# TensorE's order in a graph kernel: the fourth group's sum placed inside the linear layer, and the picked rows ahead of the self rows' transposes

## The chip, the cores and the metric

The kernel runs on one core of a Trainium2 chip. The metric is the device time of one execution in microseconds, the median of several runs. Five engines work side by side from their own instruction streams and meet at semaphores: TensorE (PE), VectorE (DVE), ScalarE (ACT), GpSimd (POOL) and SyncE (SP, which here issues DMAs). Matmuls write PSUM, which DVE and ACT read.

## The reference

One layer of a graph network over 6,250 nodes with 128 features, 106,250 edges, three edge types and three node types.

```python
parts = [relu(x)]
for t in range(3):                                  # edge types
    msg = relu(x[src] @ W_e[t].T + b_e[t])
    msg = where(edge_type == t, msg, 0)
    parts.append(segment_sum(msg, dst, 6250))
agg = concatenate(parts, axis=1)                    # 6250 x 512
for t in range(3):                                  # node types
    updated = where(node_type == t, agg @ W_n[t].T + b_n[t], updated)
out = layernorm(x + updated + x)
```

The edges come sorted by `dst`; among them is one edge from each node to itself (a "self" edge).

## The kernel before, in words

A first stage (until some 110 us) computes the message of every node under every edge type, `relu(x @ W_e[t].T + b_e[t])`, and stores the 18,750 rows in DRAM as `message_table`. After it the edges are worked off in 45 iterations `j`. An iteration holds two rows of 1,080 sorted edges; most of their messages are fetched from the table by indirect DMA, 128 rows at a time, in 14 columns that form four groups of 3, 4, 3 and 4 columns.

For a group `g` of iteration `j` the engines do this:

- POOL issues the group's gathers (line 619), one per column, into `msg` (which the trace calls `tab`). The buffer is single: the gathers of group `g` for iteration `j + 1` wait until TensorE has summed group `g` of iteration `j` (`group_summed`). POOL issues them in the order of the groups.
- DVE makes the one-hot matrices of the group for the next iteration (`one_hot`, line 1116, output `work`), also after `group_summed`, and then adds the group's sum from PSUM to the accumulator (`add_sums`, line 1125, output `acc`).
- TensorE multiplies messages by one-hot (`sum_group`, line 1516), one matmul per column, into one of two PSUM banks (`AGG`), so a sum waits until the last but one was added.

Other work is laid between these sums on TensorE. The "picked rows" are edges whose source lies in a narrow range of nodes; instead of a gather they are picked from resident rows by a one-hot matmul. `dense_turn` (line 1533, ten matmuls in two sets of five) picks them, DVE multiplies by type masks (`dense_mask`, line 1204, output `order_f`), `dense_make` (lines 1546 and 1548) makes their messages, ACT applies relu (line 747), `dense_sum` (line 1555) sums them. The "early" edges (iterations up to 35) are turned (`early_turn`, 1486), made (1496) and summed (1506).

The tile of nodes that is complete is finished one or two iterations later. `finish_turn` (1577) transposes its 128 rows of `x` into a PSUM bank; ACT writes their relu to `stage` (761); `place_selfs` (1570) transposes the three types of self rows into the same bank once ACT has read it (`stage_xt`); DVE adds them to the accumulator's sums in `stage` (1269). The linear layer is `linear_open` (a bias matmul, 1586, and the part of relu(x), 1587) and `linear_types` (1595, one matmul of 384 columns for each edge type). DVE then selects by node type, adds and normalizes (`finish_h`, 1238 to 1246, and `finish_y`, 1252 and 1254).

The order on each engine is the order in which the code is written; nothing is scheduled at run time. On TensorE it is `iteration(j)` in the tensor block (lines 1604 to 1683), with `FIN = 2` and `NG = 4`, so `g == FIN + 1` is the fourth group. SP's stream (loads for the next tiles, stores) and POOL's, DVE's and ACT's are not touched by the change.

Of the kernel before, what the change touches and what calls it, by code (L numbers as in the profile page):

```python
# [35 lines left out]
N, D, T, E = 6250, 128, 3, 106250  # L36
# [29 lines left out]
FIN = 2  # L66
# [74 lines left out]
def build(nc, x, src, dst, etype, ntype, w_e, b_e, w_n, b_n, out):  # L141
# [5 lines left out]
    with ExitStack() as ctx:  # L147
# [1266 lines left out]
        def _(pe):  # L1414
# [158 lines left out]
            def finish_turn(tile, nth, loads, z=0, first=False):  # L1573
                pe.wait_ge(fin_x[z], 16 * loads)
                if not first:
                    pe.wait_ge(stage_xt[z], nth)
                pe.transpose(ps[:, FIN_XT_PS[z], 0:P], xg[:, at(tile), :].rearrange("p a d -> p (a d)"), ident[:, :]
                             ).then_inc(fin_xt[z], 1)
# [10 lines left out]
            def linear_types(nth, z, first=1, last=T):  # L1589

                lin = ps[:, LIN_PS[z], 0:T * D]
                if first == 1:
                    pe.wait_ge(stage_acc[z], nth + 1)
                for i in range(first, last + 1):
                    ins = pe.matmul(lin, stage[z][:, i, :], wn_t[:, i, :], start=False, stop=(i == T))  # L1595
                if last == T:
                    ins.then_inc(fin_lin[z], 1)
# [5 lines left out]
            def iteration(j, early=False, fin=True, extra=None, last=False, loads=None):  # L1603
                start = j == 1
                for g in range(NG):
# [57 lines left out]
                    if g == FIN:  # L1663
                        if j == 2:
                            dense_sum(2)
                        if j > 1:
                            linear_open(j - 2, first=j == 2)
                            linear_types(j - 2, 0, 1, T)
                        if fin:
                            finish_turn(j - 1, j - 1, loads, first=start)  # L1670
                        if extra is not None:
                            linear_types(extra, 1)
                    if g == FIN + 1 and fin and j > 1:
                        place_selfs(j - 1, j - 1)
                    if g == FIN and j == 1:
                        dense_turn(1)
                    if g == FIN + 1:
                        if j == 1:
                            spread_types()
                            dense_make(1)  # L1680
                            dense_sum(1)
                        if j > 1:
                            dense_turn(j + 1)

            pe.wait_ge(consts_set, 1)
# [13 lines left out]
            for j in range(1, NI - 1):  # L1699
                iteration(j, j < NE, extra=j - EXTRA_AT if EXTRA_AT <= j < EXTRA_AT + KE else None,  # L1700
                          loads=batches_up_to(j - 1))
# [38 lines left out]
```

## Time and profile before

| | |
|---|---|
| three runs | 1091.16 us median, 1078.62 to 1099.07 |
| span of the profiled execution | 1076.0 us (from its first to its last instruction; no other time is given for it) |
| busy: PE, DVE, POOL, ACT | 72%, 64%, 62%, 14% |
| gathers by POOL in the 45 iterations | 630, 943 ns each |
| mean granted clock of TensorE | 0.872 |

In the timeline rows the columns are start in us, duration in us, engine and line, operation, output and inputs, count, and in square brackets the idle time of the engine before the row with what ended it. "issue" is time without a wait that the profile shows, "remote" a releaser that it could not name. An fp32 matmul stands there as two records, so x8 are the four matmuls of a group of four columns. A matmul's end is modelled.

### The profile page before, as it was taken

The numbers are of one execution on the slowest core, as the hardware profiler recorded it, in microseconds if no ns is written. First come the engines' busy times: TensorE is split into PE (matmuls) and PEld (weight loads), VectorE is DVE, ScalarE is ACT, GpSimd is POOL, SyncE is SP. The second block draws the span as 40 slices with busy tenths as digits, with TensorE's granted clock in tenths as the row PEclk, the third lists the DMA queues.
The fourth block names the chain that finished last, engine by engine and source line by source line (L and its number), as shares of the span: only waits on it lengthen the run. The fifth ranks groups of instructions, "written<-read, shape, count | busy, mean of one in ns | idle before, by whom it ended". The sixth has DMA issues, their size and how long they took to land. (4 is left out here: it accounts for less than half of the span.)

```text
span 1076.0 us, 13097 instructions
## 1 busy us (share of the span) xinstructions
PE 771.1 (72%) x4200; PEld 611.8 (57%) x4200; DVE 683.5 (64%) x1539; ACT 149.6 (14%) x397; POOL 671.4 (62%) x718
## 2 busy tenths in 40 slices
PE   5574267777778778777676686888787786778866
PEld 3242156666666566566555565666566565566654
DVE  7997866666555656656566565656656654465645
ACT  2264101101101101100110110011011001111101
POOL 7776655666566666665666665666666666665660
PEclk9697578978898998998999988989888978898898
DMA  7476312422222223223223223223223233132320
GB/s 219 135 256 190 81 50 60 86 72 67 78 80 75 71 77 85 72 70 89 71 70 93 74 67 91 71 67 96 72 67 108 71 105 90 45 93 70 87 57 16
DMA packets 65777, 94.03 MB, mean 87 GB/s; under 512 B 16497, under 2 KB 49233, under 8 KB 65711
## 3 DMA queue, kind: packets, MB, share of 16 engines
q0 software_dynamic: 22432, 45.99, 17.2%
q1 hardware_dynamic: 40577, 43.14, 13.0%
q10 hardware_dynamic: 2702, 4.08, 1.3%
q8 instruction: 34, 0.56, 0.2%
q14 instruction: 32, 0.26, 0.1%
HBM read 80.23 MB, written 12.92 MB: 87 GB/s over the span
## 5 line engine op out<-in xcount | busy, mean ns | idle before, releaser
L619 POOL DMA_INDIRECT tab<-message_table,idx_t x630 | 594.3, 943 | 353.0 <-issue 170.4
L1116 DVE TENSOR_TENSOR work<-key_t,ps 128x378 f32<-128x378 f32 (+1 forms) x180 | 109.5, 610 | 253.1 <-remote 133.0
L1516 PE MATMUL ps<-work,tab 128*128 128x126 f32 x1260 | 197.4, 304 | 35.4 <-DVE acc L1125 20.6
L1516 PEld LDWEIGHTS ps<-work,tab 128*128 128x128 f32 x1260 | 183.3, 219 | 50.3 <-DVE acc L1125 25.5
L1546 PE MATMUL ps<-we_t,order_f 128*128 128x128 f32 x540 | 115.4, 368 | 123.2 <-DVE order_f L1204 84.1
L1546 PEld LDWEIGHTS ps<-we_t,order_f 128*128 128x128 f32 x540 | 93.3, 255 | 135.6 <-DVE order_f L1204 88.8
L1595 PE MATMUL ps<-wn_t,stage 128*128 128x384 f32 x294 | 104.6, 493 | 0.0
L1204 DVE TENSOR_TENSOR order_f<-ps,dst_raw 128x768 f32<-128x768 f32 x45 | 43.1, 957 | 71.7 <-remote 56.7
L615 POOL DMA_INDIRECT xg<-in_x,esrc_t x67 | 71.0, 1060 | 23.9 <-issue 17.7
L1595 PEld LDWEIGHTS ps<-wn_t,stage 128*128 128x128 f32 x294 | 56.3, 193 | 39.7 <-issue 3.1
L747 ACT ACTIVATE dense_f<-ps 128x256 f32<-128x256 f32 x45 | 17.2, 383 | 432.7 <-PE ps L1548 228.8
L1496 PE MATMUL ps<-we_t,xst 128*128 128x384 f32 x142 | 60.7, 554 | 20.0 <-issue 19.6
L1125 DVE TENSOR_TENSOR acc<-ps,acc 128x126 f32 x216 | 61.1, 283 | 9.3 <-PE ps L1516 8.1
L1533 PE MATMUL ps<-first_wide,tab 128*128 128x128 f32 x450 | 59.1, 279 | 4.6 <-issue 2.9
L1448 PE MATMUL ps<-we_t,work 128*128 128x384 f32 x98 | 44.7, 541 | 19.0 <-issue 10.4
L1533 PE MATMUL ps<-dense_f,tab 128*128 128x128 f32 x450 | 58.1, 277 | 0.0
L1533 PEld LDWEIGHTS ps<-first_wide,tab 128*128 128x128 f32 x450 | 54.8, 195 | 5.5 <-issue 5.5
L1241 DVE SCALAR_TENSOR_TENSOR h<-ps,mask,h 128x128 f32<-128x128 f32 x147 | 51.6, 351 | 6.2 <-PE ps L1595 0.9
L1533 PEld LDWEIGHTS ps<-dense_f,tab 128*128 128x128 f32 x450 | 54.5, 194 | 0.0
L1555 PE MATMUL ps<-first_wide,dense_f 128*128 128x216 f32 x180 | 45.9, 382 | 5.2 <-ACT dense_f L747 5.2
L1496 PEld LDWEIGHTS ps<-we_t,xst 128*128 128x128 f32 x142 | 26.7, 209 | 35.5 <-issue 26.6
L1555 PEld LDWEIGHTS ps<-first_wide,dense_f 128*128 128x128 f32 x180 | 36.8, 214 | 16.8 <-ACT dense_f L747 6.3
(231 smaller groups left out, 952.2 us busy)
## 6 DMA issues: line engine op xcount, KB each, us to landing
tab<-message_table,idx_t POOLq DMA_INDIRECT x630
message_table<-tab SPq DMA_DIRECT2D x24, 384.0 KB
dst_raw<-dense_types SPq DMA_DIRECT2D x45, 192.0 KB
wn_raw<-message_table SPq DMA_DIRECT2D x22, 384.0 KB
src_wide<-dense_lists SPq DMA_DIRECT2D x45, 128.0 KB
xg<-in_x SPq DMA_DIRECT2D x11, 256.0 KB
work<-in_x ACTq DMA_DIRECT2D x10, 256.0 KB
out<-xg SPq DMA_DIRECT2D x10, 256.0 KB
```

What stands on the lines that cost most here:

```text
L615: pool.indirect_dma_start(xg[:, q, :], None, x, bass.IndirectOffsetOnAxis(ap=rows, axis=0)).then_inc(x_gathered, 16)
L619: pool.indirect_dma_start(msg[:, slot, :], None, table, bass.IndirectOffsetOnAxis(ap=rows, axis=0)).then_inc(signal, 16)
L1116: dve.tensor_tensor(hot[:, first:first + n, :].rearrange("p c (t w) -> p c t w", w=WIN), keys.broadcast_to((P, n, T, WIN)), iota_win.rearr ...
L1125: dve.tensor_tensor(cols, sums_bank(nth).rearrange("p (t c) -> p t c", t=T), cols, ALU.add).then_inc(added, 1)
L1241: fin_link(dve.scalar_tensor_tensor(h[z][:, :], ps[:, LIN_PS[z], t * D:(t + 1) * D], mask[:, t, at(tile)], h[z][:, :], ALU.mult, ALU.add), ...
L1448: pe.matmul(ps[:, MSG_PS + i, 0:T * D], xt[:, par, i, :], we_t[:, :], start=True, stop=False)
L1496: ins = pe.matmul(ps[:, E_MSG_PS[c], 0:T * D], xst[:, c, :], we_t[:, :], start=True, stop=True)
L1516: ins = pe.matmul(sums_bank(nth), msg[:, column, :], hot[:, column, :], start=(c == 0), stop=(c == n - 1))
L1533: ins = pe.matmul(dxt_ps[:, :, s * DENSE:(s + 1) * DENSE], dx[:, (SETS - 1 - s) * DT + k, :], donehot[s][:, k, :, :], start=(k == 0), stop ...
L1546: pe.matmul(dmsg_ps[:, side, :], dxm[:, side, t, :], we_t[:, t * D:(t + 1) * D], start=(t == 0), stop=False)
L1555: ins = pe.matmul(dense_sums(side), dsel[:, side, :], dhot[:, side, :], start=True, stop=True)
L1595: ins = pe.matmul(lin, stage[z][:, i, :], wn_t[:, i, :], start=False, stop=(i == T))
```

## The change

For `j > 2` and all but the last iteration it moves instructions on TensorE and does nothing else. The number of instructions stays the same.

```diff
                         if j > 1:
                             linear_open(j - 2, first=j == 2)
-                            linear_types(j - 2, 0, 1, T)
-                        if fin:
+                            linear_types(j - 2, 0, 1, T if j == 2 else 1)
+                        if fin and j < 3:
                             finish_turn(j - 1, j - 1, loads, first=start)
                         if extra is not None:
                             linear_types(extra, 1)
+                    if g == FIN + 1 and j > 2:
+                        linear_types(j - 2, 0, 2, T)
+                        finish_turn(j - 1, j - 1, loads)
+                        dense_turn(j + 1)
                     if g == FIN + 1 and fin and j > 1:
                         place_selfs(j - 1, j - 1)
...
-                        if j > 1:
+                        if j == 2:
                             dense_turn(j + 1)
```

TensorE's stream from the linear layer's first type to the next iteration's first sum (the wait on `gathered3` opens the fourth group's sum, the one on `gathered0` the next first group's; the words in brackets are semaphores), before:

```order
L1595 MATMUL ps<-wn_t,stage 128x384 [waits stage_acc0]
L1595 MATMUL ps<-wn_t,stage 128x384 x2
L1577 MATMUL ps<-ident,xg 128x128 [waits stage_xt0,fin_x0]
L1516 MATMUL ps<-work,tab 128x126 [waits gathered3,added]
L1516 MATMUL ps<-work,tab 128x126 x3
L1570 MATMUL ps<-ident,wn_raw 128x128 [waits stage_xt0,self_masked0]
L1570 MATMUL ps<-ident,wn_raw 128x128 x2
L1533 MATMUL ps<-first_wide,tab 128x2x64 [waits d_onehot,d_added]
L1533 MATMUL ps<-first_wide,tab 128x2x64 x4
L1533 MATMUL ps<-dense_f,tab 128x2x64 [waits d_onehot]
L1533 MATMUL ps<-dense_f,tab 128x2x64 x4
L1516 MATMUL ps<-work,tab 128x126 [waits gathered0,added]
```

The same place of the changed kernel:

```order
L1595 MATMUL ps<-wn_t,stage 128x384 [waits stage_acc0]
L1516 MATMUL ps<-work,tab 128x126 [waits gathered3,added]
L1516 MATMUL ps<-work,tab 128x126 x3
L1595 MATMUL ps<-wn_t,stage 128x384 x2
L1577 MATMUL ps<-ident,xg 128x128 [waits stage_xt0,fin_x0]
L1533 MATMUL ps<-first_wide,tab 128x2x64 [waits d_onehot,d_added]
L1533 MATMUL ps<-first_wide,tab 128x2x64 x4
L1533 MATMUL ps<-dense_f,tab 128x2x64 [waits d_onehot]
L1533 MATMUL ps<-dense_f,tab 128x2x64 x4
L1570 MATMUL ps<-ident,wn_raw 128x128 [waits stage_xt0,self_masked0]
L1570 MATMUL ps<-ident,wn_raw 128x128 x2
L1516 MATMUL ps<-work,tab 128x126 [waits gathered0,added]
```

The fourth sum moved ahead of two matmuls of the linear layer and one transpose; the picked rows' ten matmuls moved ahead of the three transposes of the self rows. In all 41 changed iterations the piece reads like this. The streams of DVE, ACT, POOL and SP are the same.

## Rows read from the trace of the kernel before

**Rows 1.** The page, head and part 1: busy time (share) xinstructions of each engine.

```profile
span 1076.0 us, 13097 instructions
...
PE 771.1 (72%) x4200; PEld 611.8 (57%) x4200; DVE 683.5 (64%) x1539; ACT 149.6 (14%) x397; POOL 671.4 (62%) x718
```

**Rows 2.** Waits: engine line, waited for: us in total, times, longest.

```profile
DVE work L1116 <- remote: 133.0, 48, 4.4
DVE work L1116 <- PE ps L1516: 117.3, 42, 4.6
POOL tab L619 <- remote: 98.5, 55, 3.3
```

**Rows 3.** Timeline of POOL around two stops, 720 to 737 us.

```profile
723.63 0.94 POOL L619 DMA_INDIRECT tab<-message_table,idx_t  x1 [1.80 <-remote]
...
731.12 0.94 POOL L619 DMA_INDIRECT tab<-message_table,idx_t  x1 [0.30 <-issue]
733.81 0.94 POOL L619 DMA_INDIRECT tab<-message_table,idx_t  x1 [1.75 <-PE ps L1516]
```

**Rows 4.** Timeline of PE, 720 to 738 us.

```profile
727.20 2.10 PE L1595 MATMUL ps<-wn_t,stage 128*128 128x384 f32 x6
729.13 0.27 PE L1577 MATMUL ps<-ident,xg 128*128 128x128 f32 x1
729.24 1.05 PE L1516 MATMUL ps<-work,tab 128*128 128x126 f32 x8
730.13 0.49 PE L1570 MATMUL ps<-ident,wn_raw 128*128 128x128 f32 x3
730.46 1.28 PE L1533 MATMUL ps<-first_wide,tab 128*128 128x128 f32 x10
...
732.69 0.83 PE L1516 MATMUL ps<-work,tab 128*128 128x126 f32 x6
```

**Rows 5.** Timeline of DVE, 722 to 738 us.

```profile
726.26 0.29 DVE L1125 TENSOR_TENSOR acc<-ps,acc 128x126 f32 x1
...
729.53 0.81 DVE L1195 TENSOR_TENSOR dense_f<-src_wide,ps 128x640 f32<-128x640 f32 x1
733.57 0.68 DVE L1116 TENSOR_TENSOR work<-key_t,ps 128x504 f32<-128x504 f32 x1 [3.23 <-PE ps L1516]
...
735.07 0.96 DVE L1204 TENSOR_TENSOR order_f<-ps,dst_raw 128x768 f32<-128x768 f32 x1 [0.62 <-remote]
...
736.60 0.54 DVE L1269 TENSOR_TENSOR stage<-acc,ps 128x384 f32<-128x384 f32 x1
```

**Rows 6.** Timeline of ACT, 722 to 738 us.

```profile
729.44 0.28 ACT L761 ACTIVATE stage<-ps 128x128 f32<-128x128 f32 x1 [1.99 <-PE ps L1577]
```

**Rows 7.** Timeline of PE, 505 to 518 us: a second sum.

```profile
510.73 1.05 PE L1516 MATMUL ps<-work,tab 128*128 128x126 f32 x8
```

**Rows 8.** Timeline of POOL, 508 to 517 us.

```profile
516.32 0.94 POOL L619 DMA_INDIRECT tab<-message_table,idx_t  x1 [1.76 <-remote]
```

**Rows 9.** Timeline of POOL, 319 to 320 and 460 to 464 us.

```profile
319.26 0.94 POOL L619 DMA_INDIRECT tab<-message_table,idx_t  x1 [1.76 <-remote]
...
462.63 0.94 POOL L619 DMA_INDIRECT tab<-message_table,idx_t  x1 [1.82 <-PE ps L1516]
```

**Rows 10.** Timeline of POOL, 476 to 507 us: a short stop and three long ones.

```profile
481.68 0.94 POOL L619 DMA_INDIRECT tab<-message_table,idx_t  x1 [0.33 <-remote]
...
488.99 0.94 POOL L619 DMA_INDIRECT tab<-message_table,idx_t  x1 [2.61 <-remote]
...
495.94 0.94 POOL L619 DMA_INDIRECT tab<-message_table,idx_t  x1 [3.51 <-PE ps L1516]
...
506.13 0.94 POOL L619 DMA_INDIRECT tab<-message_table,idx_t  x1 [1.76 <-remote]
```

**Rows 11.** Timeline of DVE, 478 to 491 us.

```profile
481.44 0.68 DVE L1116 TENSOR_TENSOR work<-key_t,ps 128x504 f32<-128x504 f32 x1 [1.82 <-remote]
...
488.68 0.96 DVE L1204 TENSOR_TENSOR order_f<-ps,dst_raw 128x768 f32<-128x768 f32 x1 [6.36 <-remote]
```

## The prediction, made before the changed kernel ran

> **What bounds the kernel now.** I read the page first: no engine is full, PE is busy 72% of the 1076.0 us and POOL 62% [rows 1]. Next the waits: DVE's one-hots of line 1116 wait 133.0 us for a releaser without a name and 117.3 us for TensorE's sums, and POOL's gathers wait another 98.5 us in 55 stops [rows 2]. So the kernel is bound by a ring of signals between POOL, PE and DVE. What the ring costs is read from the timelines of one ordinary iteration.
>
> The iteration takes 20.48 us: POOL's gathers behind the fourth sum start at 319.26 and, seven iterations later, at 462.63 [rows 9]. POOL issues seven gathers at a pitch of 1.25 us ((731.12 - 723.63) / 6), ends them at 732.06, stands still for 1.75 us and starts again at 733.81; the stop before was 1.80 us [rows 3]. Two series and two stops make an iteration. The first stop ends with the second group's sum, the other with the fourth group's.
>
> The fourth sum is the point of the change. TensorE shows it at 729.24 for 1.05 us, so ended at 730.29 [rows 4]. DVE, free since 730.34, takes up the one-hot that waits for it only at 733.57 [rows 5], and POOL goes on at 733.81 [rows 3]. Between the shown end of the sum and its effect lie 3.28 us. For the transpose just ahead of it there is no such gap: it ends at 729.40 and ACT starts on its result at 729.44 [rows 4, 6]. So what is late is the signal (or the real end) of the sum, and the question is what holds it.
>
> **What the change does, part by part.** All in one iteration, 41 times, on the rows of TensorE [rows 4].
>
> The sum moves ahead of two of three types and one transpose. The three types take 729.13 - 727.20 = 1.93 us, two of them 1.29, the transpose 0.11 (729.24 - 729.13): the sum starts at 727.84 and is shown ended at 728.89, 1.40 us earlier. Nothing holds its start: the addition that frees its bank ends at 726.55 [rows 5], 1.29 us before.
>
> The other types and `finish_turn` come later by the sum's 0.89 us (730.13 - 729.24). DVE reads the linear layer only after the next iteration's second sum, some ten us later: no cost. The transpose is shown at 730.02 and ACT's copy takes 0.28 us [rows 6], so `stage` would be there at about 730.6.
>
> The picked rows end earlier by the 0.33 us of `place_selfs` (730.46 - 730.13), and `place_selfs` follows at 732.36; DVE reads it at 736.60 [rows 5]. Ahead of it now stands a wait on ACT's copy with 1.7 us in hand. Behind that wait is queued the next first sum, shown at 732.69 as before. If the transpose's signal were held as the fourth sum's is, until about 733.57, `place_selfs` would wait to 733.9 and the first sum would end near 734.9; its reader on DVE stands behind the mask that ends at 736.03 [rows 5], so I take 0. That mask is the cover. If it were gone, the wait would cost up to 1.2 us (733.9 - 732.69), 49 us in 41 iterations; nothing here gains.
>
> The picked rows' mask starts at 735.07, 0.62 us after DVE is free [rows 5]; 0.33 us of it may go. It feeds the second sum, whose stop is the other one.
>
> What then is 1.40 us on the fourth sum worth? The bound on one side: POOL's stop goes from 1.75 to the usual 0.30 between gathers, 1.45 us, times 41 is 59 us. On the other side nothing, if the signal doesn't follow the sum. The nearest row decides for nothing. At 510.73 TensorE ran a second group's sum unusually early, shown ended at 511.78 [rows 7], and POOL started only at 516.32, after a stop of 1.76 us [rows 8]. There 4.54 us lie between the end of the sum and POOL's start, at 730.29 and 733.81 it was 3.52 us, yet the stops are 1.76 and 1.75 us [rows 3, 8]. A sum that was done a microsecond earlier shortened nothing: the signal seems to come at a fixed time after POOL's own series of seven gathers has ended. I take 0 for the sum's move.
>
> The Trainium skill ("Perfetto Trace Analysis", Per-instruction lifecycle, Tensor Engine Instruction) says that the shown end of a matmul is an estimate and that its semaphore update follows the write's acknowledgement, outside of the shown window. The transpose's 0.04 us agrees, the fourth sum's 3.28 us shows how far outside it may be. By that rule alone the signal belongs to the matmul and moves with it, which is the first rival below.
>
> The sum: 0 for the fourth sum, 0 for the moved transposes, at most a few tenths in single iterations at the end, where TensorE itself is late: about -1 us. Against the profiled execution: 1076.0 - 1 = 1075. The median of the runs is 15.2 us above that span (the fastest run 2.6 us), so 1090 us in the runs' measure.
>
> **The rivals.**
>
> *The signal follows the sum* (faster). Then DVE makes the fourth one-hot right at 730.34, POOL loses its stop, and the picked rows' mask can start when `dense_turn` is done instead of at 735.07, so that the second sum keeps up. Full price 59 us: 1032. The second stop would grow by part of it where DVE and TensorE can't follow, since TensorE's sequence up to the first sum is as long as before; with half to all of the 1.45 us I take 45 us: 1046. For it: the names in the waits, TensorE's sum as POOL's releaser; and that the sum would now stand earlier in the series of gathers (5.3 us after its start at 723.63) than any held one I looked at, while the transpose at 5.8 us passed at once [rows 3, 4, 6]. Against it: rows 7 and 8. Chance 0.30.
>
> *The signal gets through too early, and later ones are held longer* (slower). In one place the trace shows what happens when POOL does not stop after seven: at 481.68 it went on after 0.33 us and issued four more gathers, then stood 2.61 and 3.51 us [rows 10]; the picked rows' mask came 7.24 us after the fourth one-hot (488.68 - 481.44) [rows 11] instead of 1.50 (735.07 - 733.57) [rows 5]. From 462.63 to 506.13 two iterations took 43.50 us [rows 9, 10] against 40.96 for two ordinary ones: 2.54 us lost. The price is that, and it decides as soon as the fourth sum's signal comes within the 8.4 us of the series. In every second changed iteration it is 20 x 2.54 = 51 us: 1142; in one of four 25 us: 1116. For it: an earlier sum makes just this likelier. Against: it has to be frequent to count. With the 1.2 us of a wait in front of `place_selfs` in some iterations it is about the same size. Chance 0.24.
>
> *The forecast*: the stops stay, within 2%. Chance 0.46.
>
> **How the numbers follow.** About 2%, 22 us, is what a measurement of this kernel can tell from no change (its three runs span 20 us). Faster by over 2% (under 1069) takes the first rival, 0.30; slower (over 1113) the second, 0.24; between them 0.46. The range for 8 in 10 runs from 1042, which leaves out the first rival's last part down to 1032, to 1130, which takes in the second with an occurrence in one of three iterations. The forecast's own range is 1075 to 1105, that of the runs before.
>
> **What would show it.** In the profile after: POOL's stops behind the fourth sum still 1.7 to 1.9 us and the fourth one-hot still waiting, now some 4.7 us after the shown end of its sum: right. Those stops down to 0.3 us, with iterations of 19 us: the first rival. Series of eleven gathers without a stop, followed by stops over 2.5 us and a mask 5 us or more behind the fourth one-hot: the second. An idle TensorE ahead of line 1570 would show that ACT's copy is late and the cover thin. Most of all the prediction would be wrong if what I read as held by POOL's series were only TensorE's own lateness.

## The result: 4.4% slower, and the profile after

Median after 1142.72 us (1130.19 to 1152.82, 4 runs), before 1093.63 us (1078.62 to 1099.07, 4 runs), ratio 1.0439, 95% interval 1.0379 to 1.0499. Two of after's four runs (1148.03 and 1152.82 us) belong to a slower state of the chip with a lower granted clock, and the ratio leaves them out; the other two took 1130.19 and 1137.42 us. The forecast was 1090 us and its range ended at 1130; the slower rival gave 1142. The profiled execution grew from 1076.0 to 1128.4 us. First the page of after, its head and its line of busy times [rows 1]:

```profile
span 1128.4 us, 13097 instructions
...
PE 799.5 (71%) x4200; PEld 641.1 (57%) x4200; DVE 684.2 (61%) x1539; ACT 150.3 (13%) x397; POOL 671.8 (60%) x718
```

DVE and POOL did the same work to a microsecond. PE ran the same 4200 instructions in 28 us more, at a mean granted clock of 0.819 against 0.872. So for POOL and DVE the 52.4 us are waiting. First one wait of before, then the waits of after (us in total, times, longest), and the page's group of POOL's gathers, of before and then of after:

```profile
DVE order_f L1204 <- remote: 56.7, 32, 6.4
```

```profile
DVE order_f L1204 <- remote: 218.0, 38, 8.8
ACT stage L761 <- remote: 213.1, 30, 10.4
POOL tab L619 <- PE ps L1516: 136.0, 48, 10.6
PE ps L1546 <- DVE order_f L1204: 123.4, 37, 6.6
```

```profile
L619 POOL DMA_INDIRECT tab<-message_table,idx_t x630 | 594.3, 943 | 353.0 <-issue 170.4 <-remote 98.5 <-PE ps L1516 80.1
```

```profile
L619 POOL DMA_INDIRECT tab<-message_table,idx_t x630 | 594.4, 943 | 400.8 <-issue 173.7 <-PE ps L1516 136.0 <-remote 91.1
```

POOL idles 47.8 us more: that is nearly all of the 52.4. Where, its timeline shows. In one iteration of after, number 33, the gathers run from 867.06 to 880.47 without a stop:

```profile
867.06 0.94 POOL L619 DMA_INDIRECT tab<-message_table,idx_t  x1 [3.36 <-PE ps L1516]
...
879.53 0.94 POOL L619 DMA_INDIRECT tab<-message_table,idx_t  x1 [0.30 <-issue]
883.13 0.94 POOL L619 DMA_INDIRECT tab<-message_table,idx_t  x1 [2.66 <-remote]
...
890.04 0.94 POOL L619 DMA_INDIRECT tab<-message_table,idx_t  x1 [3.47 <-PE ps L1516]
```

That is a series of eleven gathers (a "series" is a row of gathers 0.30 us apart, a "stop" the longer gap behind it), a stop of 2.66 us, three gathers, a stop of 3.47 us, where before had seven, 1.80, seven, 1.75 [rows 3]; 22.98 us against 20.48. It is the pattern of rows 10. I counted the series in POOL's timelines (a gap over 0.56 us ends one): before has 5 of eleven and 74 of seven, after 21 of eleven and 35 of seven.

The loss is not spread over the 41 changed iterations. I counted POOL's gathers off against the iterations: POOL reaches the second group of iteration 16 at 456.17 us, 3.8 us later than in before (452.38), that of iteration 35 at 890.04, 43.5 us later (846.58), and the last one's 51.5 us later. From iteration 10 to 16 after keeps before's time, but not its pattern: the stops of its two series of seven stand behind the first and the third group's sums, no longer behind the second and the fourth. Iteration 10 begins at 329.57, and these are its third group's first gather and the next iteration's first:

```profile
339.86 0.94 POOL L619 DMA_INDIRECT tab<-message_table,idx_t  x1 [1.86 <-PE ps L1516]
...
350.04 0.94 POOL L619 DMA_INDIRECT tab<-message_table,idx_t  x1 [1.75 <-remote]
```

From iteration 17 to 37 nearly every one is long, some 23 us. The first of this row begins with three gathers and a stop of 3.17 us behind a second sum that took 1.91 us (477.44 to 479.35), and only then comes a series of eleven (479.62). So a series of eleven and a late second sum seem to bring each other about; which comes first is not the same everywhere (in before, at 472.92, it was the eleven).

TensorE in iteration 33 [rows 4]:

```profile
871.27 1.05 PE L1516 MATMUL ps<-work,tab 128*128 128x126 f32 x8
872.16 1.46 PE L1595 MATMUL ps<-wn_t,stage 128*128 128x384 f32 x4
873.45 0.27 PE L1577 MATMUL ps<-ident,xg 128*128 128x128 f32 x1
...
874.68 1.28 PE L1533 MATMUL ps<-dense_f,tab 128*128 128x128 f32 x10
878.83 0.52 PE L1570 MATMUL ps<-ident,wn_raw 128*128 128x128 f32 x3 [2.87 <-ACT stage L761]
...
883.78 1.65 PE L1546 MATMUL ps<-we_t,order_f 128*128 128x128 f32 x6 [3.77 <-DVE order_f L1204]
...
887.85 1.91 PE L1516 MATMUL ps<-work,tab 128*128 128x126 f32 x8
```

And its readers on DVE and ACT [rows 5, 6]:

```profile
874.85 0.68 DVE L1116 TENSOR_TENSOR work<-key_t,ps 128x504 f32<-128x504 f32 x1 [1.08 <-remote]
878.40 0.28 ACT L761 ACTIVATE stage<-ps 128x128 f32<-128x128 f32 x1 [7.53 <-remote]
882.77 0.96 DVE L1204 TENSOR_TENSOR order_f<-ps,dst_raw 128x768 f32<-128x768 f32 x1 [7.04 <-remote]
```

Three results of TensorE reach their readers late. The fourth sum, shown ended at 872.32, is taken up at 874.85 (2.53 us, of which DVE was busy for all but the last 1.08), in the middle of POOL's series, so POOL is free to issue on. The transpose of `finish_turn` is shown ended at 873.72, ACT starts at 878.40 (4.68 us). The picked rows are done at 875.96, and the mask starts at 882.77, 6.81 us later and 2.30 us behind the end of the eleven. The iteration is that chain: 13.41 us of series (867.06 to 880.47), 2.30 to the mask, 7.27 from the mask to POOL's start at 890.04 behind the second sum; together 22.98. In before the same chain, from the mask at 735.07 to the end of the second sum at 740.94, lies under seven gathers (733.81 to 742.24); here only three are left to cover it. Its second sum in before:

```profile
739.89 1.05 PE L1516 MATMUL ps<-work,tab 128*128 128x126 f32 x8
```

One row more, of the stretch behind the mask in after (columns: us, busy us and instructions of PE, PEld, DVE, ACT, POOL, then the granted clock, DMA share, GB/s):

```profile
883.00:890.00 7.00, 6.22 (x27) 5.54 (x28) 5.43 (x9) 0.77 (x2) 2.83 (x3) 0.50 0.10 28
```

Granted clock 0.50, the 1.2 GHz level, after TensorE stood idle for 3.77 us: the second sum takes 1.91 us instead of 1.05 in before. From the mask's start to the second sum's end it is 6.99 us here (882.77 to 889.76) and 5.87 in before, for the same instructions. An estimate from these rows: 1.12 of the 2.50 us that an iteration loses are the clock's, since here that chain lies open, and the rest is waiting for the signals. Fillers that raise the clock are tried in the last experiments.

### The profile page after: what moved, and what is told of

Read it like the earlier page. It is cut to its first block and busy times, and to the rows that moved or that the text cites. A ratio compares the mean times of both kernels' runs of the same rounds, so it can differ in the third digit from the quotient of the medians.

```text
span 1128.4 us, 13097 instructions
## 1 busy us (share of the span) xinstructions
PE 799.5 (71%) x4200; PEld 641.1 (57%) x4200; DVE 684.2 (61%) x1539; ACT 150.3 (13%) x397; POOL 671.8 (60%) x718
## 5 line engine op out<-in xcount | busy, mean ns | idle before, releaser
L1516 PE MATMUL ps<-work,tab 128*128 128x126 f32 x1260 | 203.8, 311 | 30.4 <-DVE work L1116 23.0
L1546 PE MATMUL ps<-we_t,order_f 128*128 128x128 f32 x540 | 125.2, 392 | 136.2 <-DVE order_f L1204 123.4
L1516 PEld LDWEIGHTS ps<-work,tab 128*128 128x128 f32 x1260 | 195.0, 227 | 44.8 <-DVE work L1116 23.2
L1546 PEld LDWEIGHTS ps<-we_t,order_f 128*128 128x128 f32 x540 | 102.0, 277 | 149.4 <-DVE order_f L1204 131.2
L1204 DVE TENSOR_TENSOR order_f<-ps,dst_raw 128x768 f32<-128x768 f32 x45 | 43.1, 957 | 226.7 <-remote 218.0
L1595 PE MATMUL ps<-wn_t,stage 128*128 128x384 f32 x294 | 110.1, 490 | 0.0
L1496 PE MATMUL ps<-we_t,xst 128*128 128x384 f32 x142 | 71.1, 636 | 8.5 <-issue 7.9
L1595 PEld LDWEIGHTS ps<-wn_t,stage 128*128 128x128 f32 x294 | 53.1, 192 | 28.5 <-issue 1.2
L1570 PE MATMUL ps<-ident,wn_raw 128*128 128x128 f32 x132 | 24.2, 296 | 54.9 <-issue 42.5
L761 ACT ACTIVATE stage<-ps 128x128 f32<-128x128 f32 x49 | 13.6, 277 | 309.2 <-remote 213.1
L1506 PE MATMUL ps<-ehot,esel 128*128 128x126 f32 x142 | 34.8, 390 | 20.7 <-DVE esel L1170 16.1
```

Source lines behind the costliest of these rows:

```text
L1204: dve.tensor_tensor(dxm, dxt_ps.rearrange("p i (o e) -> p i o e", o=1).broadcast_to((P, 2, T, P)), dtypes[:, j % 2, :].rearrange("p (i t e ...
L1496: ins = pe.matmul(ps[:, E_MSG_PS[c], 0:T * D], xst[:, c, :], we_t[:, :], start=True, stop=True)
L1516: ins = pe.matmul(sums_bank(nth), msg[:, column, :], hot[:, column, :], start=(c == 0), stop=(c == n - 1))
L1546: pe.matmul(dmsg_ps[:, side, :], dxm[:, side, t, :], we_t[:, t * D:(t + 1) * D], start=(t == 0), stop=False)
```

## The experiments

Each ratio is to the kernel before, run on the same chip between. A difference under 2% counts as the same, and where the 95% interval crosses 2% the verdict is unclear.

**e1, the sum alone.** After, with the old order of picked rows and transposes:

```diff
-                        dense_turn(j + 1)
                     if g == FIN + 1 and fin and j > 1:
                         place_selfs(j - 1, j - 1)
+                    if g == FIN + 1 and j > 2:
+                        dense_turn(j + 1)
```

> After, with the self rows' transposes put back ahead of the picked rows: of the change only the fourth group's sum is moved. Theory A: TensorE's signals are held back while POOL issues its gathers one behind the other, and the early fourth sum lets POOL issue eleven in one row, which delays the fourth sum's own signal, the self rows' transposes and the picked rows alike. The sum's move alone then costs all of it: 1135 to 1150 us, iterations of 23 us from the sixteenth on, and DVE's mask (L1204) held 7 us or more. Rival B: ScalarE's copy of the types, now later, and the self rows that wait for it hold the picked rows, and the order of the two decides: with the old order it would be worse than after by up to 1.2 us an iteration, 1160 to 1190 us. Rival C: the swap of picked rows and transposes is what costs; then this one is at 1085 to 1100 us.

Measured: 1109.9 us, 1.0214 (1.0134 to 1.0295), unclear at 2%. No theory had it: the sum's place alone costs about half of the loss. Iterations mostly alternate, about 20.1 and 22.5 us; series of eleven are rare (3). The rows of a longer one, DVE, ACT and POOL:

```profile
563.00 0.68 DVE L1116 TENSOR_TENSOR work<-key_t,ps 128x504 f32<-128x504 f32 x1 [3.37 <-remote]
```

```profile
563.12 0.28 ACT L761 ACTIVATE stage<-ps 128x128 f32<-128x128 f32 x1 [6.38 <-remote]
```

```profile
560.41 0.94 POOL L619 DMA_INDIRECT tab<-message_table,idx_t  x1 [0.30 <-issue]
563.24 0.94 POOL L619 DMA_INDIRECT tab<-message_table,idx_t  x1 [1.89 <-remote]
...
570.00 0.94 POOL L619 DMA_INDIRECT tab<-message_table,idx_t  x1 [2.07 <-PE ps L1516]
```

The fourth sum is shown ended at 558.18, and both results get through only at 563.0 to 563.1, 1.7 us behind the end of the seven gathers (561.35). Only then can the self rows' transposes run, and the picked rows behind them. And TensorE, idle for 3.96 us, runs these at the low clock (the last three numbers of the second row: granted clock, DMA share, GB/s):

```profile
564.21 2.34 PE L1533 MATMUL ps<-first_wide,tab 128*128 128x128 f32 x10
```

```profile
563.54:568.68 5.14, 5.14 (x24) 5.14 (x25) 0.34 (x2) 0.00 (x0) 3.47 (x4) 0.50 0.16 42
```

The picked rows take 4.47 us (564.21 to 568.68) where before has 2.40 (730.46 to 732.86). So some 2 us of such an iteration, most of what it is longer by, are the clock after an idle stretch, and the idle stretch comes from the held signals.

**e2, the swap alone.** Before, with the picked rows ahead of the transposes:

```diff
+                    if g == FIN + 1 and j > 2:
+                        dense_turn(j + 1)
                     if g == FIN + 1 and fin and j > 1:
                         place_selfs(j - 1, j - 1)
```

> Before, with only the picked rows put ahead of the self rows' transposes from the third iteration on; the fourth sum stands where it stood. Theory A (signals held while POOL issues; the fourth sum's place makes the long row of gathers): 1080 to 1100 us, within 1% of before, since the swap gives the picked rows 0.3 us and nothing in POOL's rows changes. Rival C (the swap costs): 1125 to 1145 us.

Measured: 1084.33 us, 0.9935 (0.9894 to 0.9976): the same at 2%, as theory A had it, with an interval just below 1, and the lowest ratio of all versions that do the whole work. Its trace has 83 series of seven and one of eleven; ordinary iterations are 20.7 us, longer than before's 20.48, and there are fewer disturbed ones. Where the small gain comes from the traces can't show: the traced run of e2 has a span of 1084.5 us, and that of before, its fastest run, 1076.0. The product of e1 and e2 is 1.015, the change as a whole 1.044: the two parts harm each other, by some 31 us, clear of the three intervals.

**e4, half a dose.** After, with the sum behind two of the three types:

```diff
-                            linear_types(j - 2, 0, 1, T if j == 2 else 1)
+                            linear_types(j - 2, 0, 1, T if j == 2 else 2)
...
-                        linear_types(j - 2, 0, 2, T)
+                        linear_types(j - 2, 0, 3, T)
```

> After, with the fourth group's sum behind the second of the three types instead of the first: 0.65 us later. Theory A (whether POOL issues on without a stop is a matter of when the fourth sum's signal gets out against POOL's row of gathers): a threshold, so the time is near after's (1130 to 1145) if 0.65 us is too little to restore the stop, and 1090 to 1100 if it is enough; both kinds of iteration may be in one run, 1100 to 1125. Rival D (the time goes with the later types and the later ScalarE copy, in proportion): halfway, 1115 to 1120, with every iteration longer by half as much as in after (1.2 us).

Measured: 1124.85 us, 1.0313 (1.0257 to 1.0369), at the upper end of theory A's mixed case, 5 us above rival D's. Its iterations are not all longer by half: they mix 20.5 with 23.5 to 24.6 us, with 8 series of eleven. So it is a mixture, as theory A had it, and D's even lengthening falls; the time alone would not have told them apart.

**e3, a wait on POOL.** After, and in `gpsimd`, ahead of the fourth group's gathers:

```diff
+                    if j > 3 and g == NG - 1:
+                        pool.wait_ge(d_turned, j + 1)
```

> After, and POOL waits for the picked rows' signal (d_turned) before the fourth group's gathers, from the fourth iteration on: one wait more, nothing else. Theory A (the mask is late because the picked rows' signal is held while POOL issues; a stop of POOL lets it through): the row of eleven gathers is cut in seven and four, the mask starts some 3 us behind the picked rows instead of 7, and the time is 1085 to 1115 us although POOL has a wait more. Rival B (TensorE's own work is late, and POOL's issue is no cause): POOL loses the stop, 1.5 to 2.5 us an iteration, on top: 1145 to 1200 us.

Measured: 1197.11 us, 1.0968 (1.0882 to 1.1054). The time is rival B's, and my forecast for theory A missed by 82 us. The trace shows both reasons, in the rows of PE, DVE and POOL:

```profile
724.45 2.07 PE L1535 MATMUL ps<-dense_f,tab 128*128 128x128 f32 x10
```

```profile
726.55 0.96 DVE L1206 TENSOR_TENSOR order_f<-ps,dst_raw 128x768 f32<-128x768 f32 x1 [2.99 <-PE ps L1535]
```

```profile
727.29 0.95 POOL L619 DMA_INDIRECT tab<-message_table,idx_t  x1 [4.40 <-PE ps L1535]
```

With POOL standing, the picked rows (L1535 here) are shown ended at 726.52 and the mask starts at 726.55: 0.03 us instead of 6.81. Rival B, TensorE late by itself, falls by this row, though its time came. But POOL now stands 4.40 us for them in nearly every iteration, and the iteration is 24 us. And the wait did not cut the series in seven and four, as I expected: the fourth group's gathers, the next first and the next second group's now make one series of eleven (727.29 to 740.74), 35 of them in the run.

**e6, e7, e8: what in POOL's work is it?** Before, with the gathers of iterations 25 to 34 replaced; these kernels fetch other rows there, so the messages of the ten iterations are wrong. e6: SyncE issues plain copies behind the same waits, and TensorE waits for them:

```diff
+                    sp.wait_ge(group_summed, NG * (j - 1) + g + 1)
+                    for column in range(FIRST_COLUMN[g], FIRST_COLUMN[g] + SLOTS[g]):
+                        sp.dma_start(msg[:, column, :], table[column * P:(column + 1) * P, :]).then_inc(copied[g], 16)
```

> Before, with the 14 gathers of each of ten iterations (25 to 34, some 640 to 850 us) replaced by as many plain copies of 128 rows of the same table into the same buffers, issued by SyncE on its own queue; POOL only waits in that stretch. The bytes and their destination stay, the rows are other ones (the messages of these ten iterations are wrong). Theory A1 (what holds TensorE's signals is POOL's issue of gathers): in the stretch DVE's one-hots start within 0.1 us of the shown end of the sum they wait for, ACT's copies likewise, and the iteration is bound by TensorE and DVE, 15 to 19 us. Theory A2 (it is the transfers' traffic into the buffers): the gaps of 1 to 4 us between a shown end and its effect stay as they are, and the iterations stay at 20 us or longer. Rival B (TensorE is late by itself): the gaps stay too.

e7 adds on POOL, in the place of a group's gathers:

```diff
+                        fill(3 * SLOTS[g])      # pool.memset(pause[:, :], 0.0), each after the one before
```

> As the one with SyncE's copies in iterations 25 to 34, and POOL, which waits for the same sums as before, does three memsets of a scratch tile (128x256) in the place of each gather of that stretch (some 1 us each three): POOL is as busy as before but issues no DMA. The messages of these ten iterations are wrong as there. Theory A1 (POOL's issue of gathers holds the signals): no gaps, as without the memsets, iterations within 1 us of theirs. Theory E (any work of POOL holds them): the gaps of 1 to 4 us between a shown end and its effect are back, and iterations are 19 us or longer.

e8, in the place of a gather:

```diff
+                            pool.dma_start(msg[:, column, :], table[column * P:(column + 1) * P, :]).then_inc(gathered[g], 16)
```

> Before, with the 14 gathers of each of ten iterations (25 to 34) replaced by plain copies of 128 rows of the same table, issued by POOL itself; the messages of these ten iterations are wrong. SyncE's copies in that place left no gap between a shown end and its effect, and iterations of 15.3 us. Theory A1a (what holds the signals is POOL issuing any DMA from its software queue): gaps of over 1 us are back in the stretch, wherever POOL issues, with iterations over 17 us. Theory A1b (it is the gather's own work, the offsets read from memory and one row per descriptor): no gaps, as with SyncE's copies, iterations of 15 to 17 us.

Measured: 1027.71, 1033.56 and 1031.11 us in single runs. In all three the mask of one iteration follows that of the last after 15.32 us in that stretch, where before takes 20.5. e6, in the order of time, PE and DVE:

```profile
710.59 1.05 PE L1529 MATMUL ps<-work,tab 128*128 128x126 f32 x8
...
712.92 1.28 PE L1546 MATMUL ps<-dense_f,tab 128*128 128x128 f32 x10
```

```profile
698.92 0.96 DVE L1217 TENSOR_TENSOR order_f<-ps,dst_raw 128x768 f32<-128x768 f32 x1 [1.68 <-PE ps L1546]
...
711.68 0.68 DVE L1129 TENSOR_TENSOR work<-key_t,ps 128x504 f32<-128x504 f32 x1 [0.19 <-PE ps L1529]
...
714.24 0.96 DVE L1217 TENSOR_TENSOR order_f<-ps,dst_raw 128x768 f32<-128x768 f32 x1 [1.68 <-PE ps L1546]
```

The sum ends at 711.64 and is taken up at 711.68, the picked rows at 714.20 and 714.24. The gaps of 3.3 us are gone, though the transfers run at a higher rate. The windows (columns as above) of e6 inside the stretch and of before:

```profile
685.00:760.00 75.00, 67.52 (x439) 55.70 (x438) 62.84 (x139) 11.08 (x35) 0.00 (x0) 1.00 0.39 103
```

```profile
640.00:845.00 205.00, 159.28 (x890) 130.74 (x889) 127.56 (x277) 22.14 (x70) 131.13 (x140) 0.88 0.29 79
```

So it is not the amount of traffic (103 against 79 GB/s). The granted clock is higher too, 1.00 against 0.88; how much of the 5.2 us less it gives was not tried apart. It is not POOL being busy either: e7's POOL is full of memsets, and the mask still starts 0.04 us behind the picked rows (shown ended 711.45):

```profile
699.97 16.91 POOL L637 MEMSET pause<- 128x256 f32 x45
```

```profile
711.49 0.96 DVE L1229 TENSOR_TENSOR order_f<-ps,dst_raw 128x768 f32<-128x768 f32 x1 [1.68 <-PE ps L1558]
```

And not a DMA that POOL issues: e8's plain copies hold nothing (picked rows shown ended 707.99, mask 708.03), which is A1b and against A1a.

```profile
708.03 0.96 DVE L1208 TENSOR_TENSOR order_f<-ps,dst_raw 128x768 f32<-128x768 f32 x1 [1.68 <-PE ps L1537]
```

**e17, half the rows.** Before, in the same ten iterations `msg[0:64, column, :]` from the first 64 of each column's rows.

> Before, with each gather of iterations 25 to 34 taking 64 rows instead of 128 (the lower half of each message tile keeps old rows, so the messages there are wrong). Theory A with the descriptor's count as the cause: the held signals get out sooner, stops of POOL fall well below the 1.8 us, if the gather's own 0.94 us on POOL gets shorter too. Theory A with the mere instruction as the cause: gathers stay at 0.9 us and 1.25 us pitch, and stops at 1.7 to 1.9 us, iterations at 20.5 us.

Measured: 1094.73 us in one run. A gather falls from 0.94 to 0.90 us only, and the stops don't shrink:

```profile
726.75 0.90 POOL L634 DMA_INDIRECT tab<-message_table,idx_t  x1 [2.14 <-remote]
```

The iterations of the stretch don't get shorter either: many alternate between about 19.7 and 22.9 us, where I had expected 20.5. It is the indirect gather as such, hardly the number of its rows: shown for 64 against 128, no further, and in one run.

**e5, e10, e11: a pause in POOL's row.** After, ahead of the fourth group's gathers from the fourth iteration on, n memsets of a scratch tile, n = 4, 6, 2:

```diff
+                    if j > 3 and g == NG - 1:
+                        fill(4)
```

> After, with four memsets of a scratch tile (128x256, each waits for the one before) on POOL between the third and the fourth group's gathers, from the fourth iteration on: POOL gets some 1.5 to 2.5 us of work more in each of 41 iterations, but issues no gather in that time. Theory A (TensorE's signals are held while POOL issues gathers): the row of eleven is cut in seven and four, the picked rows' mask and the self rows' transposes get their signals in the gap, the idle ahead of L1204 falls from 218.0 us by more than half, and the time falls to 1085 to 1120 us in spite of the extra work. Rival B (POOL's issue is no cause, TensorE is late by itself): the memsets lie on the ring, +1.5 to 2.5 us an iteration, 1180 to 1240 us. Rival E (it is POOL's being busy with anything, not its gathers): the signals are held through the memsets too, 1150 to 1200 us.

> After, with six memsets in the place of the four of the kernel with POOL's pause (some 2.15 us instead of 1.43). There the trace showed why four gained only half: held signals came 1.7 us behind the end of the series of seven, and at 697.39 POOL had gone on before the picked rows' signal was out, which then waited for the end of the next series. Theory A: six memsets outlast that, the mask comes within 2 us of the series' end in nearly every iteration, and an iteration is 8.43 + 2.15 + 8.43 + 1.9 = 20.9 us: 1085 to 1105 us, faster than with four memsets although POOL works 30 us more. Rival H (a pause only shifts where the long series stand, and every us of it counts): 1115 + 41 x 0.72 = 1145 us, 1130 to 1150.

> After, with two memsets (some 0.7 us) in the place of four. Theory A: 0.7 us behind the series' end nothing held is out yet (it comes 1.6 to 1.7 us behind it), so the pause lets no signal through, the idle ahead of L1204 stays near after's 218 us, and the time is after's or up to 20 us above: 1130 to 1165 us. Rival H (a shorter pause is a cheaper one): less than with four memsets, 1090 to 1112 us.

Measured: n = 4 1115.4 us, 1.0222 (1.018 to 1.0264); n = 6 1112.48, 1.021 (1.0148 to 1.0273); n = 2 1108.36, 1.0154 (1.0065 to 1.0242). All three beat after's 1.0439 although POOL has up to 77 us more to do, which no theory of a full POOL allows; n = 4 lies in theory A's range. But the doses missed: two memsets should have let nothing through, yet they gained as much as four or six (the intervals overlap), and DVE's unnamed wait ahead of the mask fell from 218.0 to 56.4 us in all; and six did not reach 1105. The trace of n = 6, POOL, PE and DVE:

```profile
731.47 2.17 POOL L626 MEMSET pause<- 128x256 f32 x6
733.79 0.95 POOL L630 DMA_INDIRECT tab<-message_table,idx_t  x1 [0.15 <-issue]
```

```profile
730.65 1.28 PE L1546 MATMUL ps<-dense_f,tab 128*128 128x128 f32 x10
```

```profile
733.37 0.96 DVE L1217 TENSOR_TENSOR order_f<-ps,dst_raw 128x768 f32<-128x768 f32 x1 [1.53 <-PE ps L1546]
```

The picked rows, ended at 731.93, reach DVE in the pause, 1.44 us later, as expected; every second iteration still has a series of eleven elsewhere, and the two kinds take 21.0 and 21.8 us, not 20.9. That the signals come in a gap is shown; how the gap's length maps to time is not understood. Rival H's times (1130 to 1150 for n = 6, 1090 to 1112 for n = 2) came for n = 2 and not for n = 6.

**e9, does TensorE's further work matter?** e1, with 20 transposes of a constant where its TensorE waits for ACT's copy:

```diff
                         finish_turn(j - 1, j - 1, loads)
+                        pe.wait_ge(d_added, 2 * (j + 1))
+                        for _ in range(20):
+                            pe.transpose(ps[:, DENSE_PS, 0:P], ident[:, :], ident[:, :])
```

> The kernel with the sum's move alone (the self rows' transposes ahead of the picked rows), with 20 transposes of a constant (some 2 us) on TensorE behind the transpose of finish_turn, where that kernel's TensorE stands idle for about 4 us until ACT's copy is done; their result is overwritten. Theory F (a held signal gets out within POOL's series only if TensorE goes on working behind it, so that the swap's picked rows are what lets the fourth sum's signal out and makes the series of eleven): series of eleven are back in most iterations, over ten of them, against one or two with the idle TensorE, and the time goes to 1125 to 1150 us. Rival G (what TensorE does behind the sum has no part in it; the series of eleven come from where the picked rows stand in the chain): series of eleven stay rare and the time stays at 1105 to 1120 us, since the 20 transposes fill a gap.

Measured: 1148.98 us, 1.055 (1.0466 to 1.0633), 14 series of eleven against 3: theory F's numbers. It is the likely way in which the two parts of the change harm each other: with the picked rows right behind `finish_turn` TensorE works on while the fourth sum's signal is held, and then that signal comes in the middle of POOL's series. It isn't shown beyond the count, since the transposes also cost TensorE 2.2 us of their own ahead of the picked rows, and e12 below gets slower by such a filler as well. In a stretch of e9 something else shows, single matmuls standing apart; first POOL's last gather of a series of eleven, then TensorE:

```profile
738.35 0.94 POOL L619 DMA_INDIRECT tab<-message_table,idx_t  x1 [0.30 <-issue]
```

```profile
739.27 0.27 PE L1533 MATMUL ps<-dense_f,tab 128*128 128x128 f32 x1 [0.74 <-issue]
739.97 0.48 PE L1533 MATMUL ps<-dense_f,tab 128*128 128x128 f32 x2 [0.43 <-issue]
740.66 0.37 PE L1533 MATMUL ps<-dense_f,tab 128*128 128x128 f32 x1 [0.21 <-issue]
```

They start 0.70 us apart, within some two microseconds behind the end of the series at 739.29, where ten of them else follow in 1.28 us. Here it is TensorE itself that is late, and the mask (742.33) follows the shown end of the picked rows (742.29) by 0.04 us. So a late result need not be a held signal alone: a matmul that is shown ended may not have ended yet, and these runs don't tell the two apart.

**e12 to e15, the clock behind the mask.** n transposes of a constant between the next first sum and the wait for the mask; after with n = 30 and 16, the swap alone (e2) and before with 20:

```diff
                         if j > 2:
+                            after_next = sums_ahead(j, 1)
+                            pe.wait_ge(added, after_next - len(AGG) + 1)
+                            for _ in range(30):
+                                pe.transpose(ps[:, AGG[after_next % len(AGG)], 0:P], ident[:, :], ident[:, :])
                             dense_make(j)
```

> After, with 30 transposes of a constant (some 3.3 us at the high clock, their result overwritten) on TensorE between an iteration's first sum and its wait for DVE's mask, where it stands idle for 3.77 us in after (880.01 to 883.78); from there to 890 us its granted clock was 0.50. Theory K (the lost time is the clock: the chain from the mask to POOL's start, 7.27 us, holds some 2.6 us of matmuls at 1.2 GHz, and only after's chain lies open there): the matmuls of L1546 take 0.94 us instead of 1.65, iterations of 20.4 to 21 us where they were 23.0: 1080 to 1105 us. Theory A alone (held signals, the clock a by-product): the signals come no sooner and the chain is 0 to 1 us shorter: 1125 to 1145 us. Rival M (the transposes hold the mask's messages up where the mask is early, as in the first half): above 1145.

> The same with 16 transposes instead of 30 (some 1.8 us), so that TensorE still stands idle for some 2 us behind them in an iteration of the long series. Theory K: the clock is helped in part, 1095 to 1125 us, and the time goes with the granted clock of the chain. Theory A alone: 1130 to 1145 us.

> The swap alone (picked rows ahead of the self rows' transposes, sum where it stood), with 20 such transposes (2.2 us) in the same place. There the signals of the sums end POOL's stops at a fixed 1.9 us behind each series of seven and the chain from the mask is covered by POOL's seven gathers. Theory A: no gain, 1080 to 1092 us, since nothing of the chain lies open. Theory K in its strong form (the clock sets the iteration everywhere): 1050 to 1070 us.

> Before, with 20 such transposes in the same place. In before the messages of L1546 also run at the low clock (1.65 us for six), but the chain behind them ends at 740.94, before POOL's series at 742.24. Theory A: no gain in ordinary iterations, and at most the four disturbed ones (2.54 us each) are shorter: 1078 to 1092 us. Theory K in its strong form: 1045 to 1070 us.

Measured: e12 1168.88 us, 1.0743 (1.0674 to 1.0812); e13 1094.81, 1.013 (1.006 to 1.02); e14 1090.98, 1.0044 (1.0014 to 1.0074); e15 1096.3, 1.0112 (1.0075 to 1.015). Theory K in its strong form falls: where the chain is covered, a mean of 0.29 us for a matmul of L1546 instead of 0.37 gains nothing. In after 16 transposes win back two thirds of the loss (theory K's side, just below its 1095) and 30 add to it. e13 doesn't show that the clock was the cause, since the transposes also left only 3 series of eleven. e12's time is rival M's, and matmuls stand 0.70 us apart there again, late in a series and behind one.

**e16, the same without gathers.** e6 (so with other rows in those ten iterations) with the 30 transposes.

> The kernel with SyncE's copies in iterations 25 to 34, with the 30 transposes of the filled kernels between the first sum and the mask's messages in every iteration. In the filled kernels TensorE's matmuls stood apart by 0.7 us each in some stretches late in a series of gathers (single matmuls of L1516 with 0.45 us idle ahead), once much was queued. Theory A (POOL's gathers hold back TensorE's completions, and with many of them outstanding TensorE itself stalls): in iterations 25 to 34, without gathers, the 30 transposes run back to back in 3.3 to 3.7 us and no matmul stands apart; an iteration takes 15.3 plus 2 to 3.5 us. Rival N (TensorE stalls by its own instruction stream, when there are many instructions): the same gaps of 0.4 us and more are in that stretch as well.

Measured: 1068.19 us in one run. In the stretch without gathers they run back to back, the picked rows (shown ended 733.93) reach the mask after 0.04 us, and masks follow at 16.55 us:

```profile
734.43 3.44 PE L1667 MATMUL ps<-ident 128*128 128x128 f32 x30
```

```profile
717.42 0.96 DVE L1217 TENSOR_TENSOR order_f<-ps,dst_raw 128x768 f32<-128x768 f32 x1 [1.68 <-PE ps L1546]
733.97 0.96 DVE L1217 TENSOR_TENSOR order_f<-ps,dst_raw 128x768 f32<-128x768 f32 x1 [1.68 <-PE ps L1546]
```

Rival N falls. An iteration costs 1.23 us more than in e6, less than the 2 I had as the least.

## Why the prediction was wrong, step by step

**The failed step** is "I take 0 for the sum's move", with the reading under it that "the signal seems to come at a fixed time after POOL's own series of seven gathers has ended". e1 prices the move at 2.1% (19 us between the medians, 23 by the ratio), and with the swap it is 49 us. The reading holds where the sum stands as in before: e2's ordinary stops are 1.9 to 2.0 us. But it is a statement about a signal held by a running series, and I used it as if the series were given, each stop tied to its group. Once the sum ends earlier, at 872.32 or 5.3 us into the series, its signal can come inside it, and then POOL doesn't stop and the series itself gets longer, or its stops move to other groups (iterations 10 to 16, at no cost). The price then comes from the two stops that stay, 2.66 and 3.47 us, and from the clock behind the long idle stretch, which my sum had nowhere. Rows 10 and 11 had this in full, and rows 7 and 8, from which I took the 0, showed a second group's sum, not the fourth.

**The bounds.** I bounded the move from +0 to a gain of 59 us and left the loss to a rival. The loss has no place between them: with a signal that is held for longer, the other side of an earlier sum is not "nothing".

**The slower rival** was right in mechanism and in the price of one occurrence: 2.54 us, against 22.98 - 20.48 = 2.50. That its 1142 for "every second changed iteration" meets the median of 1142.72 is partly luck: it had no argument on how frequent, and the two runs in the ratio took 1130.19 and 1137.42 us. What the traces count: iterations over 22.5 us are 24 in after and 4 in before, 20 more, but in one row from the 17th on and not every second. There were 16 series of eleven more than before, at 2.5 us 40 of the 52 us; other long iterations have broken series instead (seven, four and three gathers, 640.16 to 663.23, 23.07 us), and 3.6 us were lost by iteration 4. I gave it 0.24 since "it has to be frequent to count". The range even left out its stronger half.

**The faster rival** fell, though POOL did lose its stop behind the fourth sum. In an iteration POOL won 1.45 us (the stop of 1.75 down to 0.30) and gave back 2.36 at the next first sum (0.30 to 2.66) and 1.67 at the second (1.80 to 3.47).

**`place_selfs` and its cover.** "1.7 us in hand" was wrong: ACT starts 4.68 us behind the shown end of its transpose, TensorE waits for it (2.87 us at L1570), as the last "what would show it" said. It seems to cost nothing by itself here, since the first sum's signal, too, has to wait for the series' end; no run tries it alone. "That mask" as cover was no cover at all, as it waits for the same held signals.

**The swap**, priced at 0 to 0.33 us, was right alone (0.9935), and wrong in company: I added the parts of the change as if each had its own time. e9 suggests that what TensorE does behind the sum bears on when the sum's signal gets out.

The Trainium skill ("Perfetto Trace Analysis", Per-instruction lifecycle, Tensor Engine Instruction) puts the semaphore update outside of the matmul's shown window. The runs agree, with 0.04 us without gathers and up to 6.81 with them; the section gives no size, and in these runs the distance goes with what POOL issues and not with the matmul.

Open: what in the gather holds TensorE, whether it holds the signal or the matmul's real end, why a held result sometimes gets out within a series (872.32 in after) and sometimes not (558.18 in e1, as deep in its series), and the clock's share in after beyond the estimate of 1.12 us an iteration.

## What to carry to other kernels

Where the trace shows an engine's results late by microseconds, find first what the other engines issue in that time, and treat the lateness as a state that the change can alter: bound the move of such a result on both sides with the worst stretch that the profile of before already has. Parts of a change that touch one ring of signals are not to be added; run each alone. And where a ring is bound by held signals, a little idle time or filler in the right place can be worth more than the time it costs (after with 2 memsets or 16 transposes a round), but try the dose. Look at the granted clock of the stretch behind every such wait: in e1 and after TensorE, idle for want of a signal, then did its work slower on the same chain.

## What the runs showed of the hardware

- With POOL issuing indirect gathers one behind the other (0.94 us each, 1.25 us pitch), results of TensorE that end some 5 us or more into the series reach DVE, ACT and POOL late, often 1.7 us behind the end of a series of seven and 2.3 behind one of eleven (561.35 to 563.0, 880.47 to 882.77), some of them within it (a transpose, shown ended at 873.72, at 878.40), and now and then at once (before's transpose, 729.40 to 729.44). With plain copies in their place, issued by SyncE or by POOL, or with memsets, it is 0.04 us.
- Gathers of 64 rows take 0.90 us on POOL, those of 128 rows 0.94, and hold TensorE's results as well.
- With more work queued (e9, e12), TensorE's matmuls start 0.70 us apart late in such a series or within some two microseconds behind it.
- After TensorE stood idle for 3.77 us in after and 3.96 us in e1 its granted clock was 0.50 in the stretch that follows: eight records of a sum took 1.91 us instead of 1.05, ten of the picked rows 2.34 instead of 1.28.
- Without gathers the same iteration takes 15.32 us instead of 20.48, at a granted clock of 1.00.
